# Layer-2 transposes moved from TensorE to DMA, projections moved early, sixth expert ahead of the next scores

## The chip, the core and the metric

The kernel runs on one NeuronCore of a Trainium2 chip. The metric is the device time of one execution in microseconds; the time before is the median of three runs. Engines are called by their short names: PE (TensorE, matmuls and transposes by matmul), DVE (VectorE), ACT (ScalarE), POOL (GpSimd) and SP (SyncE, which here only issues DMAs). Each has its own in-order instruction stream; they meet through semaphores. "Us" are microseconds from the start of the profiled span.

## The reference

A residual network of two layers on x [32 sequences x 64 tokens, 512], with a context of the same shape:

```python
x = x + L0_xattn(layernorm(x), ctx)   # 32 heads of 128, 8 key/value heads, biases
x = x + L0_ffn(layernorm(x))          # relu(x Wup)^2 Wdown + latent experts scaled by top-2 gate; layernorm
x = x + L1_xattn(layernorm(x), ctx)   # rmsnorm inside; 32 heads of 16, 8 key/value heads
x = x + L1_ffn(layernorm(x))
# L1_ffn: logits = x Wg + bg; y_e = relu(x W_e + b_e), e = 0..7; mean of the two experts with the top logits
```

The L1 FFN is computed densely: all 8 experts for every token, then a mask.

## The kernel before

**Numbers.** Each fp32 operand of a matmul is split into two fp16 parts, "hi" (a copy cast to fp16) and "lo" (the remainder); a product is three matmuls (hi hi, hi lo, lo hi), which `group3` issues. So one operand of [128 x 512] takes an ACT copy, a DVE subtraction, and for use as the contracted side eight 128 x 128 transposes (four blocks, two parts).

**Tiles and stages.** The 2048 tokens are 16 tiles of 128 rows (NT = 16), in 4 chunks of 4 tiles (TC = 4). Stages in time: layer-1 attention by head group and chunk (to about 1004 us); layer-1 FFN by chunk (`ffn_chunk(0)` to `ffn_chunk(2)`, then `ffn_last(3)`, in which tiles 0 and 1 of layer-2 attention already run); then `attn_step(n)` for n = 1 to 15, one tile of layer-2 attention each, interleaved with experts of tiles n - 2 and n - 1; last the experts of tile 15. The order of each engine is written out by hand, and the steps below are in that order.

**A layer-2 step on PE** (L1045): experts 6 and 7 of tile n - 2 with `scores(n, 1)` between; `tile_turn` of the normed tile n - 1 (L651 to L661: 8 transposes into a PSUM bank, stored to SBUF by ACT's `tile_store`, L665); `gate(n - 1)`; expert 0; `tile_turn` of the normed tile n + 1; `weigh_v(n, 0)` (probabilities times V, first half); expert 1; `project(n + 1)` (query, key, value); `weigh_v(n, 1)`; expert 2; `turn_o(n)` (attention output turned by PE); expert 3; `output(n)`; expert 4; `scores(n + 1, 0)`; expert 5. Each expert is 12 matmuls of 512 columns into bank 2 or 3 by turns; expert e waits until DVE has evacuated expert e - 2.

**The same step on DVE**: `less_max(n, 0)` (two row maxima L1973, two subtractions L1977), expert 5 of n - 2 (evacuation with bias, L1941), `ffn_lo(n - 1)` (L646: the lo part of the FFN's normed input), expert 6, `row_sums` (L1983), reciprocals, `probs_lo` (L1995), expert 7, `less_max(n, 1)`, `mask_of(n - 1)` (top two of the gate), `row_sums` and `probs_lo` of half 1, expert 0 of n - 1, `out_scale(n, 0)` (L2004), `out_lo` (L2010), reciprocals, expert 1, `norm_stats` of tile n + 2 (L673), `out_scale(n, 1)`, `out_lo`, `q_lo(n + 1)` (L1947), expert 2, `kv_lo(n + 1)` (L1954, L1958, L1963), `norm_apply` (newton from L594, L686) and `tile_lo` (L646) of tile n + 2, expert 3, `add_out(n)` (L2015, residual add and statistics), expert 4, `norm_apply(n)` for the FFN.

**ACT** takes exponentials (L1424) and their fp16 copy (L1430, which waits until the turn of the half before has read the buffer), the relu of each expert with its mask (L1389), `out_hi` (L1443), `project_hi` (L1396 to L1404), `turned_o` (L1448) and the copies of the normed tiles (L651). **POOL** adds experts 1 to 7 into `acc` (L578) and the sum into X (L581).

**SP** already turns queries (two issues, L427), keys (L431) and probabilities (L436) of tiles n >= 2 by DMA: `turn_p(n, 0)`, `store_out(n - 2)`, `turn_p(n, 1)`, `turn_q(n + 1)`, `turn_k(n + 1)`, each behind the semaphores of what it reads and overwrites. `turn_p(n, b)` waits for `probs_lo(n, b)` and for the `weigh_v` before it, since the turned probabilities have one buffer. A turn of probabilities is 16 blocks, one of keys 8.

**The FFN chunk** (L909): 12 jobs of 512 rows, then for each of 4 tiles `ffn_down` and `ffn_fc2`; meanwhile DVE makes the next chunk's normed tiles, and after tiles 0 and 1 PE turns two of them each, through two staging buffers `xs[:, 0]` and `xs[:, 1]`.

Of the kernel before, what the change touches and what calls it, by code (L numbers as in the profile page):

```python
# [22 lines left out]
F16 = mybir.dt.float16  # L23
# [6 lines left out]
P = 128  # L30
# [40 lines left out]
def build(nc, x, ctxT, wB, wX, biasB, bo, gam, bet, lnw, be, bg, w_split, out):  # L71
    with ExitStack() as stack:
# [43 lines left out]
        xs = R4[:, 0:2048].rearrange("p (i s d) -> p i s d", i=2, s=2)  # L116
        XT = R1.rearrange("p (c s k n) -> p c s k n", c=NC, s=2, k=KC)
# [33 lines left out]
        T2 = [parts(R4, 2048, KC, P), parts(R4, 3072, KC, P)]  # L151
        def heads(cols):
            return cols.rearrange("p (h s d) -> p h s d", h=32, s=4)
# [22 lines left out]
        def phalves(cols):  # L176
# [8 lines left out]
                     b_tp=((4, 5), (4, 5)), b_pv=6, b_to=7, b_y=0)  # L185
        TILE1 = REST._replace(qT=qturned(R3[:, 3072:4096].bitcast(F16)), kT=kturned(R3[:, 1024:1536].bitcast(F16)),
# [25 lines left out]
        def home(n):  # L212
            if isinstance(n, int) and n < 2:
                return (TILE0, TILE1)[n]
            return REST
# [4 lines left out]
        const_in, gb_in, out_done = sem("const_in"), sem("gb_in"), sem("out_done")  # L220
# [7 lines left out]
        n_bn, n_mv, n_arg, n_ln, n_r0, n_a, n_a2, n_b, n_r = (sem("n_" + s) for s in "bn mv arg ln r0 a a2 b r".split())  # L228
        n_xn, n_hi, n_lo, n_turned, n_stored = (sem("n_" + s) for s in "xn hi lo turned stored".split())
# [13 lines left out]
        a_q, a_qhi, a_qlo, a_kv, a_kvhi, a_klo, a_kdup = (sem("a_" + s) for s in "q qhi qlo kv kvhi klo kdup".split())  # L243
        q_in, k_in, pr_in = [sem("q_in0"), sem("q_in1")], sem("k_in"), sem("pr_in")
# [11 lines left out]
        wq_in, wkv_in, wo_in, g1_in = sem("wq_in"), sem("wkv_in"), sem("wo_in"), sem("g1_in")  # L256
# [21 lines left out]
        def attn_turn(n):  # L278
            return n * 2 + 31 if not isinstance(n, int) or n > 0 else 28
# [11 lines left out]
        def ffn_turn(n):  # L291
            return n * 2 + 34 if not isinstance(n, int) or n < NT - 1 else 63
# [8 lines left out]
        def _(sp):  # L301
# [66 lines left out]
            sp.dma_start(gamb, gam.broadcast_to([P, D])).then_inc(gb_in, 16)  # L368
            sp.dma_start(betb, bet.broadcast_to([P, D])).then_inc(gb_in, 16)
# [16 lines left out]
            ready(SMALL, 1568, 32, g1w, 0, 32, g1_in)  # L386
# [6 lines left out]
            ready(FC2KV, 1024, 1024, AW, 4096, 1024, wkv_in)  # L393
# [29 lines left out]
            def turn_q(n):  # L423
                sp.wait_ge(a_qlo, n + 1)
                sp.wait_ge(b_s, n * 2)
                for b in range(2):
                    sp.dma_start_transpose(REST.qT[:, b], REST.qs[64 * b:64 * b + 64].rearrange("p h s d -> p (h s d)")).then_inc(q_in[b], 16)  # L427
# [9 lines left out]

            def store_out(n):
# [18 lines left out]
        def _(pool):  # L457
# [112 lines left out]
            g.memset(REST.V[64:P, :, 1, :], 0.0).then_inc(z_ready, 1)  # L570

# [70 lines left out]
        def tile_lo(dve, n, par, src, turned=None):  # L642
# [3 lines left out]
            nc.vector.tensor_tensor(xs[:, par, 1, :], src, xs[:, par, 0, :], ALU.subtract).then_inc(n_lo, 1)  # L646

        def tile_hi(act, n, par, src, turned=None):
            act.wait_ge(n_xn, n + 1)
            w(act, n_turned, n - 1 if turned is None else turned)  # L650
            nc.scalar.activation(xs[:, par, 0, :], src, ACT.Copy).then_inc(n_hi, 1)  # L651
# [52 lines left out]
        def _(pe):  # L704
# [78 lines left out]
            def ffn_job(c, q):  # L783
# [3 lines left out]
                if isinstance(c, int) and c == 0 and kind != UP:  # L787
                    pe.wait_ge(*((fc1_in, 16) if kind == FC1 else (ex_in, 32)))
# [120 lines left out]
            def ffn_chunk(c):  # L909
                n = chunk_first(c)  # L910
                ahead = c == 2
                for q in range(12):
                    ffn_job(c, q)
                    if ahead and q == 6:
                        tile_turn(pe, attn_turn(0), 0, 4, attn_turn(0))
                    if ahead and q == 8:
                        for arrived in (wq_in, wkv_in, wo_in, g1_in):
# [1276 lines left out]
```

## Time and profile before

| | |
|---|---|
| median of 3 runs | 1830.26 us (1821.8 to 1833.26) |
| the profiled execution | 1821.84 us, its span 1820.0 us |
| busy: PE, DVE, ACT, POOL | 1711.9, 1226.9, 758.5, 485.7 us |
| mean granted clock of PE | 0.988 of full |

The span is what the trace covers. A busy PE is not PE at its peak, and idle time of an engine that is not the bound costs nothing; so the views that matter are those that say what each wait waited for. Rows of the timeline overlap a little, since an instruction starts before the last has drained.

### The profile page before, as it was taken

To read this page: it belongs to the slowest core of one execution; us is meant where nothing else is said; L and a number is where in the kernel's file an instruction comes from. 1 tells how busy PE (TensorE), PEld (TensorE's weight loads), DVE (VectorE), ACT (ScalarE), POOL (GpSimd) and SP (SyncE) were. 2 spreads that over 40 slices of the span, in tenths; PEclk is the share of its full clock that TensorE was granted. 3 is DMA by queue.
4 is the path that set the end of the run, shared out by engine and by line. 5 is a ranking of instruction groups with operands and counts; after the bars stand their busy time and mean duration, and the time that the engine had idled before them with its cause. 6 is when DMAs were issued, how large, how long until landed. Compare 5 with 4: busy or idle time off the path is not lost.

```text
span 1820.0 us, 32614 instructions
## 1 busy us (share of the span) xinstructions
PE 1711.9 (94%) x12832; PEld 907.5 (50%) x12832; DVE 1226.9 (67%) x2352; ACT 758.5 (42%) x1335; POOL 485.7 (27%) x370
## 2 busy tenths in 40 slices
PE   5889999999999999999998999998899999999997
PEld 2445555555555555555554444444454444444443
DVE  5776656655665656465657577776878878877863
ACT  5443333333333333333334333343555555545542
POOL 0152650704407025066000000000122322322324
PEclk9899999999999999999999999999999999999999
DMA  6122241412404114035311300002433333333230
GB/s 237 36 59 70 76 145 24 160 27 59 128 13 139 50 45 146 18 93 174 93 37 24 122 1 1 1 1 105 150 71 65 58 65 64 59 65 64 57 66 12
DMA packets 188976, 131.08 MB, mean 72 GB/s; under 512 B 172832, under 2 KB 173088, under 8 KB 180896
## 3 DMA queue, kind: packets, MB, share of 16 engines
q1 hardware_dynamic: 121248, 112.28, 21.4%
q10 hardware_dynamic: 67584, 16.79, 5.3%
q8 instruction: 102, 1.67, 0.4%
q14 instruction: 42, 0.34, 0.1%
HBM read 65.60 MB, written 20.97 MB: 48 GB/s over the span
## 4 chain that ended last, share of the span: by engine, by line
PE 64%; DVE 17%; DMA 7%; ACT 7%; issue 5%; DVEq 0%; ACTq 0%; POOL 0%; SPq 0%; POOLq 0%
PE bank L716 59%; DMA R<-R 7%; PE bank L762 3%; DVE R L1995 2%; DVE smx L1983 2%; ACT R L1430 2%; ACT R L1187 1%; DVE smx L1973 1%; DVE smx L1643 1%; PE bank L658 1%; PE bank L1010 1%; DVE R L1827 1%; ACT R L1338 1%; DVE AW L1645 1%; DVE bank L1977 1%
## 5 line engine op out<-in xcount | busy, mean ns | idle before, releaser
L716 PE MATMUL bank<-R 128*128 128x512 f16 (+1 forms) x7152 | 1298.9, 341 | 22.5 <-DVE R L1590 7.0
L716 PEld LDWEIGHTS bank<-R 128*128 128x128 f16 x7152 | 583.9, 98 | 666.4 <-issue 34.0
L1590 DVE SCALAR_TENSOR_TENSOR R<-bank,biases,R 128x512 f16<-128x512 f32 x288 | 204.7, 746 | 218.7 <-ACT R L1179 176.0
L578 POOL TENSOR_TENSOR R<-R 128x512 f32<-128x512 f32 x112 | 145.3, 1297 | 409.3 <-ACT R L1389 408.0
L1179 ACT ACTIVATE R<-bank,biases 128x512 f16<-128x512 f32 x128 | 87.7, 686 | 255.3 <-PE bank L716 254.5
L469 POOL TENSOR_SCALAR R<-R 128x2048 f32<-128x2048 f32 (+1 forms) x20 | 32.9, 1646 | 416.3 <-PE bank L716 351.5
L1389 ACT ACTIVATE R<-R,msk 128x512 f32<-128x512 f32 x128 | 90.5, 720 | 61.3 <-DVE R L1941 60.7
L716 PE MATMUL bank<-CT,R 128*128 128x512 f16 x384 | 94.2, 398 | 22.9 <-DVE CT L1564 11.5
L1602 DVE SCALAR_TENSOR_TENSOR R<-bank,R 64x512 f16<-64x512 f32 x64 | 44.0, 688 | 98.8 <-ACT R L1187 98.4
L1675 DVE SCALAR_TENSOR_TENSOR X<-bank,X 128x512 f32<-128x512 f32 x128 | 86.8, 683 | 32.2 <-PE bank L716 32.1
L1941 DVE SCALAR_TENSOR_TENSOR R<-bank,R 128x512 f32<-128x512 f32 x128 | 87.0, 680 | 21.4 <-PE bank L716 20.2
L1187 ACT ACTIVATE R<-bank 64x512 f16<-64x512 f32 x128 | 75.7, 591 | 54.0 <-PE bank L716 52.8
L716 PE MATMUL bank<-R,CT 128*128 128x128 f16 x1536 | 91.0, 219 | 0.0
L1214 ACT ACTIVATE AW<-AW 128x512 f32<-128x512 f32 x64 | 40.3, 630 | 120.0 <-DVE AW L1645 120.0
L716 PEld LDWEIGHTS bank<-R,CT 128*128 128x128 f16 x1536 | 88.4, 98 | 0.9
L716 PE MATMUL bank<-AW,R 128*128 128x512 f16 x384 | 88.1, 379 | 0.5 <-ACT R L1448 0.5
L1193 ACT ACTIVATE R<-bank,biases 128x512 f16<-128x512 f32 x128 | 80.8, 685 | 1.1 <-PE bank L762 1.0
L665 ACT ACTIVATE R<-bank 128x1024 f16<-128x1024 f16 x64 | 64.6, 1021 | 39.5 <-PE bank L658 39.5
L483 POOL TENSOR_TENSOR R<-R 128x512 f16<-128x512 f32 x68 | 79.1, 1193 | 1.7
L483 POOL TENSOR_TENSOR AW<-R,AW 128x512 f16<-128x512 f32 x64 | 78.5, 1258 | 1.3
L1219 ACT ACTIVATE AW<-AW 128x512 f16<-128x512 f32 x64 | 40.3, 630 | 82.5 <-DVE AW L1656 82.5
L716 PEld LDWEIGHTS bank<-CT,R 128*128 128x128 f16 x384 | 38.7, 102 | 66.3 <-issue 19.0
(156 smaller groups left out, 1724.3 us busy)
## 6 DMA issues: line engine op xcount, KB each, us to landing
R<-in_wB SPq DMA_DIRECT2D x16, 1024.0 KB, 5.6
R<-in_wX SPq DMA_DIRECT2D x16, 1024.0 KB, 4.8
w_split<-AW SPq DMA_DIRECT2D x16, 1024.0 KB, 4.9
R<-w_split SPq DMA_DIRECT2D x12, 1024.0 KB, 6.9
R<-in_ctxT SPq DMA_DIRECT2D x4, 1024.0 KB, 9.8
X<-in_x SPq DMA_DIRECT2D x4, 1024.0 KB, 13.6
out<-X SPq DMA_DIRECT2D x16, 256.0 KB, 2.0
R<-in_wB SPq DMA_DIRECT2D x7, 512.0 KB, 5.6
```

The source lines that it names most:

```text
L483: last = g.tensor_tensor(lo[:, q], src[:, q], hi[:, q], ALU.subtract)
L578: g.tensor_tensor(acc, acc, tmp[:, e % 2, :], ALU.add).then_inc(e_acc, 1)
L665: nc.scalar.activation(dst, banks16[bank][:, 0:2 * KC * P].rearrange("p (a n) -> p a n", a=2 * KC), ACT.Copy).then_inc(n_stored, 1)
L716: last = pe.matmul(dst, a(sa), b(sb_), start=(k == 0), stop=(k == m - 1))
L762: last = pe.matmul(out_v[:, :, bb, :], V[:, b, p, :], PTb[:, b * 256:(b + 1) * 256], start=(p == 0), stop=(p == 1))
L1179: sc.activation(qT[:, 0, :, j, :], banks[j % 2].rearrange("p (b l) -> p b l", l=64), ACT.Identity, bias=bias_col(g * HG, j)).then_inc(p_hi, 1)
L1187: last = sc.activation(V[64 * half:64 * half + 64, odd:BC:2, 0, :], v[64 * odd:64 * odd + 64], ACT.Copy, scale=UN)
L1193: sc.activation(oT[:, 0, :, jb * P:(jb + 1) * P], banks[6 + jb % 2].rearrange("p (h n) -> p h n", h=HG), ACT.Identity, bias=bias_col(g, 40 ...
L1389: sc.activation(dst, tmp[:, e % 2, :], ACT.Relu, scale=msk[:, 16 + e:17 + e]).then_inc(e_rel, 1)
L1590: v.scalar_tensor_tensor(out=dst, in0=src, scalar=bias, in1=hi, op0=ALU.add, op1=ALU.subtract).then_inc(done, 1)
L1675: v.scalar_tensor_tensor(out=xt, in0=banks[6 + t % 2], scalar=UN2, in1=xt, op0=ALU.mult, op1=ALU.add).then_inc(y_add, 1)
L1941: v.scalar_tensor_tensor(out=tmp[:, e % 2, :], in0=banks[2 + e % 2], scalar=UN, in1=beb[:, e, :], op0=ALU.mult, op1=ALU.add).then_inc(e_bi ...
```

## The change

1. Steady layer-2 steps (n >= 2): the normed tile for the FFN (`turn_ffn`, semaphore `fn_in`) and that for the attention (`turn_attn`, `an_in`) are turned by DMA from SP. The two `tile_turn` of PE and the two `norm_store` of ACT go. Only the attention output is still turned by PE. The turned attention input gets a buffer of its own (TA), the queries a place away from the turned probabilities (LATER, in the first part of the context, which is free by then), V a second buffer for odd tiles.
2. `project(n + 1)` moves ahead of `weigh_v(n, 0)`; `project_hi`, `q_lo` and `kv_lo` move with it. Experts 1 and 2 now lie between the two `weigh_v`, expert 3 behind them, expert 4 behind `turn_o`.
3. On PE, expert 5 of tile n - 1 moves between `output(n)` and `scores(n + 1, 0)`. On DVE and ACT expert 5 of n - 2 moves ahead of `less_max` and of the exponentials. On DVE expert 2 moves ahead of `out_scale(n, 1)`.
4. FFN chunks 0 to 2: the next chunk's four tiles get four staging buffers (`room`) and are turned by four DMAs from SP (`fx_in`); PE's turns and ACT's stores there go.
5. Step 1 becomes `step_one`: PE's turns stay, expert 5 goes ahead of `scores(2, 0)`. Some constant loads share semaphores.

```diff
+        xs_more = R3[:, 3072:4096].bitcast(F16).rearrange("p (i s d) -> p i s d", i=2, s=2)
+        def room(i):
+            return xs[:, i] if i < 2 else xs_more[:, i - 2]
+        TA = parts(R4, 10752, KC, P)
+        V_odd = vhalves(R4[:, 11776:12288])
+        LATER = REST._replace(qs=heads(CT0[:, 0:2048]))
...
 # SP
+            for c in range(NC - 1):
+                sp.wait_ge(u_mm, 12 * (c + 1))
+                for t in range(TC):
+                    sp.wait_ge(n_lo, chunk_first(c) + t + 1)
+                    sp.dma_start_transpose(T1[:, :, :, t * P:(t + 1) * P].rearrange("p s k n -> p (s k) n"),
+                                           room(t).rearrange("p s d -> p (s d)")).then_inc(fx_in[t], 16)
...
+            def turn_norm(n, sem_, par, dst):
+                sp.dma_start_transpose(dst.rearrange("p s k n -> p (s k) n"),
+                                       xs[:, par].rearrange("p s d -> p (s d)")).then_inc(sem_, 16)
+            def turn_ffn(n):
+                sp.wait_ge(n_lo, ffn_stat(n) + 1)
+                if n == 1:
+                    sp.wait_ge(a_kv, 3)
+                else:
+                    sp.wait_ge(e_mm, (n - 1) * NE)
+                turn_norm(n, fn_in, 0, T2[n % 2])
+            def turn_attn(n):
+                sp.wait_ge(n_lo, attn_stat(n) + 1)
+                sp.wait_ge(a_kv, n)
+                sp.wait_ge(b_plo, 4)
+                turn_norm(n, an_in, 1, TA)
...
             turn_k(2)
+            turn_attn(3)
             for n in range(2, NT):
+                turn_ffn(n - 1)
                 turn_p(n, 0)
                 store_out(n - 2)
                 turn_p(n, 1)
                 if n < NT - 1:
                     turn_q(n + 1)
                     turn_k(n + 1)
+                if n < NT - 2:
+                    turn_attn(n + 2)
+            turn_ffn(NT - 1)
...
 # PE, ffn_chunk
-                    if t < 2:
-                        for u in (2 * t, 2 * t + 1):
-                            tile_turn(pe, n + u, u % 2, 4 + u % 2, n + (u - 1))
-                pe.wait_ge(n_stored, n + TC)
+                for landed in fx_in:
+                    pe.wait_ge(landed, (c + 1) * 16)
...
 # PE, steady step (n >= 2), new
+                expert(n - 2, 6, last)
+                scores(n, 1)
+                expert(n - 2, 7, last)
+                gate(n - 1, this)
+                expert(n - 1, 0, this)
+                if more:
+                    project(n + 1, ctx_t, TA)
                 else:
+                    expert(n - 1, 1, this)
+                weigh_v(n, 0)
+                expert(n - 1, 1 if more else 2, this)
                 if more:
+                    expert(n - 1, 2, this)
+                weigh_v(n, 1)
+                expert(n - 1, 3, this)
+                pe.wait_ge(r_lg, n)
+                turn_o(n)
+                expert(n - 1, 4, this)
+                output(n)
+                expert(n - 1, 5, this)
                 if more:
                     scores(n + 1, 0)
...
 # ACT, steady step
+                if two:
+                    expert(n - 2, 5)
                 exponentials(n, 0)
...
+                if two:
+                    if more:
+                        project_hi(n + 1)
                     expert(n - 1, 0)
+                    if not more:
+                        expert(n - 1, 1)
+                    out_hi(n, 0)
+                    if more:
+                        expert(n - 1, 1)
+                        if has(n, -2):
+                            norm_root(act, attn_stat(n + 2), 1)
+                    expert(n - 1, 2)
+                    out_hi(n, 1)
...
 # DVE, steady step
                 if two:
+                    expert(n - 2, 5)
                     less_max(n, 0)
+                    ffn_lo(n - 1)
+                    expert(n - 2, 6)
...
                     expert(n - 1, 0)
+                if two and more:
+                    q_lo(n + 1)
                 out_scale(n, 0)
                 out_lo(n, 0)
                 reciprocals(n, 1)
-                if one:
+                if two and more:
+                    kv_lo(n + 1, not odd)
+                if more:
                     expert(n - 1, 1)
...
                     norm_stats(dve, attn_stat(n + 2), 1, x_tile(n + 2), True)
+                if two:
+                    expert(n - 1, 2)
                 out_scale(n, 1)
                 out_lo(n, 1)
```

## Rows read from the trace of the kernel before

**Rows 1.** Page, busy time; then windows: one layer-2 period, all engines, clock, DMA.
```profile
PE 1711.9 (94%) x12832; PEld 907.5 (50%) x12832; DVE 1226.9 (67%) x2352; ACT 758.5 (42%) x1335; POOL 485.7 (27%) x370
...
core 0: us, PE busy (x) PEld busy (x) DVE busy (x) ACT busy (x) POOL busy (x), PEclk, DMA share, GB/s
...
1519.70:1553.40 33.70, 31.94 (x270) 16.55 (x266) 27.15 (x64) 17.94 (x36) 10.38 (x9) 1.00 0.33 63
```
**Rows 2.** Chain that ended last, 1510 to 1550 us: start us, us, what.
```profile
1512.86 1.30 DVE smx L1973 x2
...
1520.48 4.24 DMA R<-R
1524.81 1.09 ACT R L1430 x2
...
1528.44 4.24 DMA R<-R
1532.72 0.96 PE bank L1010 x32
...
1546.48 1.30 DVE smx L1973 x2
```
**Rows 3.** Timeline of PE: start us, us, instruction, count, idle before and its releaser.
```profile
1499.09 0.96 PE L1010 MATMUL bank<-R 128*128 128x16 f16 x32 [0.51 <-DMA R<-R]
...
1521.10 0.46 PE L716 MATMUL bank<-g1w,R 128*128 128x8 f16 x12 [1.12 <-ACT R L665]
1521.42 2.75 PE L716 MATMUL bank<-R 128*128 128x512 f16 x12
```
**Rows 4.** Timeline of DVE, in two neighbouring periods.
```profile
1503.30 0.28 DVE L1954 TENSOR_TENSOR R<-bank,R 128x128 f16<-128x128 f32 x1
...
1508.93 0.68 DVE L2015 SCALAR_TENSOR_TENSOR X<-bank,X 128x512 f32 x1
1509.77 0.69 DVE L673 BATCH_NORM_STATS2 stat<-X 128x6 f32 x1 [0.15 <-DVE X L2015]
...
1515.99 0.68 DVE L646 TENSOR_TENSOR R<-yn,R 128x512 f16<-128x512 f32 x1
...
1517.74 1.29 DVE L1983 TENSOR_REDUCE smx<-bank 128x8 f32<-128x512 f32 x2 [0.42 <-ACT R L1430]
...
1528.33 0.68 DVE L1941 SCALAR_TENSOR_TENSOR R<-bank,R 128x512 f32<-128x512 f32 x1
```
**Rows 5.** DMA issues: out<-in, queue, kind, count, median us to landing.
```profile
R<-R SPq DMA_TRANSPOSE x70, 4.2
AW<-AW ACTq DMA_TRANSPOSE x64, 3.2
```
**Rows 6.** Timeline around two POOL adds: ACT, POOL and DVE.
```profile
1301.22 1.25 DVE L1963 COPY R<-R 128x384 f16<-128x384 f16 x1
...
1503.42 0.72 ACT L1389 ACTIVATE R<-R,msk 128x512 f32<-128x512 f32 x1 [0.16 <-DVE R L1941]
...
1504.31 1.31 POOL L578 TENSOR_TENSOR R<-R 128x512 f32<-128x512 f32 x1 [4.92 <-ACT R L1389]
1504.41 1.23 DVE L594 TENSOR_TENSOR stat<-stat 128x1 f32<-128x1 f32 x1
```
**Rows 7.** Timeline at the entry (DVE) and at the last tile (DVE, PE).
```profile
1309.63 1.28 DVE L1973 TENSOR_REDUCE smx<-bank 128x8 f32<-128x512 f32 x2
...
1785.11 0.98 DVE L646 TENSOR_TENSOR R<-yn,R 128x512 f16<-128x512 f32 x1 [0.70 <-ACT R L651]
...
1791.96 0.46 PE L716 MATMUL bank<-g1w,R 128*128 128x8 f16 x12 [2.00 <-ACT R L665]
```
**Rows 8.** Timeline of the FFN chunks: DVE at a boundary, PE's transposes at another.
```profile
1071.46 0.69 DVE L1827 TENSOR_TENSOR R<-R 128x512 f32<-128x512 f32 x1 [0.72 <-ACT R L1336]
...
1172.51 1.22 PE L658 MATMUL bank<-ident,R 128*128 128x128 f16 x16 [0.53 <-DVE R L646]
```
**Rows 9.** PE behind its longest layer-2 wait: timeline, then the window after it.
```profile
1601.61 0.96 PE L1010 MATMUL bank<-R 128*128 128x16 f16 x32 [2.13 <-DMA R<-R]
...
1602.40:1606.00 3.60, 3.60 (x16) 1.34 (x14) 1.54 (x3) 2.68 (x9) 0.00 (x0) 0.53 0.00 0
```

More of the change, by code:

```diff
@@ L228, in build @@
         n_bn, n_mv, n_arg, n_ln, n_r0, n_a, n_a2, n_b, n_r = (sem("n_" + s) for s in "bn mv arg ln r0 a a2 b r".split())
+        fx_in = [sem(f"fx_in{t}") for t in range(TC)]
         n_xn, n_hi, n_lo, n_turned, n_stored = (sem("n_" + s) for s in "xn hi lo turned stored".split())
@@ L243, in build @@
         a_q, a_qhi, a_qlo, a_kv, a_kvhi, a_klo, a_kdup = (sem("a_" + s) for s in "q qhi qlo kv kvhi klo kdup".split())
+        fn_in, an_in = sem("fn_in"), sem("an_in")
         q_in, k_in, pr_in = [sem("q_in0"), sem("q_in1")], sem("k_in"), sem("pr_in")
@@ new lines, in step_one @@
+            def step_one(ctx_t):
+                n = 1
+                pe.wait_ge(f_y, NT - 1)
+                tile_turn(pe, ffn_stat(0), 0, 7, ffn_turn(0))
+                turn_p(n, 0)
+                gate(0, T2[0])
+                expert(0, 0, T2[0])
+                pe.wait_ge(r_lg, n)
+                tile_turn(pe, attn_stat(2), 1, 7, attn_turn(2))
+                weigh_v(n, 0)
+                expert(0, 1, T2[0])
+                turn_p(n, 1)
+                project(2, ctx_t, T2[1])
+                weigh_v(n, 1)
+                expert(0, 2, T2[0])
+                turn_o(n)
+                expert(0, 3, T2[0])
+                output(n)
+                expert(0, 4, T2[0])
+                expert(0, 5, T2[0])
+                scores(2, 0)
@@ new lines, in attn_step @@
+            def attn_step(n, ctx_t):
+                more = n < NT - 1
+                last, this = T2[n % 2], T2[1 - n % 2]
+                expert(n - 2, 6, last)
[5 more added lines that the diff above has]
+                    project(n + 1, ctx_t, TA)
+                else:
+                    expert(n - 1, 1, this)
+                weigh_v(n, 0)
+                expert(n - 1, 1 if more else 2, this)
+                if more:
+                    expert(n - 1, 2, this)
+                weigh_v(n, 1)
+                expert(n - 1, 3, this)
+                pe.wait_ge(r_lg, n)
+                turn_o(n)
+                expert(n - 1, 4, this)
+                output(n)
+                expert(n - 1, 5, this)
+                if more:
@@ L1085, in attn_step @@
                     scores(n + 1, 0)
-                expert(n - 1, 5, T2[1 - buf])
             def ctx_tile(n):
@@ L1458, in attn_step @@
                 if two:
-                    expert(n - 2, 5)
                     expert(n - 2, 6)
-                if one:
-                    norm_store(ffn_turn(n - 1), 1 - buf)
+                if not two:
+                    norm_store(ffn_turn(0), 0)
                 if two:
@@ L1494, in attn_step @@
                     expert(n - 1, 4)
-                tile_hi(act, ffn_stat(n), 0, yn, ffn_turn(n - 1) + 1 if one else 33)
+                if two:
+                    act.wait_ge(fn_in, (n - 1) * 16)
+                tile_hi(act, ffn_stat(n), 0, yn, ffn_turn(0) + 1)
             def ffn_last(c):
@@ L2049, in attn_step @@
                     expert(n - 1, 0)
+                if two and more:
+                    q_lo(n + 1)
+                if two and not more:
+                    expert(n - 1, 1)
                 out_scale(n, 0)
@@ L2059, in attn_step @@
                     norm_stats(dve, attn_stat(n + 2), 1, x_tile(n + 2), True)
+                if two:
+                    expert(n - 1, 2)
                 out_scale(n, 1)
                 out_lo(n, 1)
-                if more:
+                if not two:
                     q_lo(n + 1)
-                if one:
                     expert(n - 1, 2)
-                if more:
                     kv_lo(n + 1)
@@ L2136, in _ @@
             ffn_last(NC - 1)
-            attn_step(1)
-            with dve.Fori(2, NT - 2) as n:
-                attn_step(n)
-            attn_step(NT - 2)
-            attn_step(NT - 1)
+            attn_step(1, True)
+            with dve.Fori(0, NT // 2 - 2) as i:
+                for k in range(2):
+                    attn_step(i * 2 + (2 + k), k == 1)
+            attn_step(NT - 2, False)
+            attn_step(NT - 1, True)
             ffn_lo(NT - 1)
```

190 lines of the change are left out of this document (79 added, 111 removed).

## The prediction

> **What bounds the kernel now.** I began with the page's shares. TensorE (PE) is busy for 94% of the span, and its granted clock is nearly full [rows 1], which invites the reading "PE is the bound, so every transpose taken off it is time won". The change acts in three stages, so I looked at each: the FFN chunks of layer 1 (about 1004 to 1215 us), the attention steps of layer 2 (n = 2 to 14, from 1309.6 us on) and the last tile.
>
> In layer 2 the work repeats. The row maxima of tile n's first half (`less_max(n, 0)`, L1973) begin at 1512.86 and, a step later, at 1546.48 [rows 2]: a period of 33.63 us. The shares give PE 31.94 us in such a period [rows 1]. The chain of waits [rows 2] is the view that decides. It doesn't run along PE. From L1973 it goes through DVE and ACT to a DMA transpose of 4.24 us (the first half's probabilities, turned from 1520.48), ACT's L1430, which may overwrite the buffer only then, DVE again, a second DMA transpose (from 1528.44), then PE's `weigh_v(n, 1)` and what follows it (an expert, `turn_o`, expert, output, expert), then DVE and L1973 of the next tile. This is a closed loop: each link waits for the one before. I call the start of L1973 L, and the start of `weigh_v(n, 1)` V. [rows 2] give V = L + 1532.72 - 1512.86 = L + 19.86.
>
> **The steady step, what PE no longer does.** Both PE transposes (L658, 8 blocks each) and the store behind them leave: 2 x 8 x 0.056 = 0.9 us of issue, the 1.12 us for which the gate waits on ACT's L665 [rows 3], and some gaps. What is left on PE, start to start: ten groups of twelve 512-wide matmuls at 2.59 (25.9; the 2.75 of a row less 0.16 that overlaps the next), the key/value projection at half that width 1.31, gate 0.31, `weigh_v` 2 x 0.82, `turn_o` 0.44, scores 2 x 0.44 [rows 3]: 30.5 us. If PE were the bound, a step would fall by 3.1.
>
> **The same step, walked along the loop.** From L to the second transpose nothing leaves the loop. `expert(n-2, 5)` used to be evacuated inside it, but there DVE waited for ACT anyway (0.42 us in front of L1983 [rows 4]); with it gone DVE waits 1.1. So V stays L + 19.86.
> From V on PE used to run expert, `turn_o`, expert, output, expert. Now it is `weigh_v` 0.82, expert 3 2.59, `turn_o` 0.44, expert 4 2.59, output 2.59 and 0.16 for the last to drain [rows 3]: output is there at V + 9.2. DVE then needs 3.93 from its residual add (L2015 at 1508.93) to the next L1973 [rows 4]. Before, it came to that add at V + 9.84 (1499.09 to 1508.93 [rows 3, 4]), held up by the query and key/value remainders; these move ahead of V, which wins 0.6. But expert 5 now stands in front of `less_max`: its evacuation, 0.60 (L1941's 0.68 less the overlap with what follows [rows 4]), is now on the loop, which costs 0.6. Sum: 19.86 + 9.23 + 3.93 + 0.60 = 33.62, against 33.63. **The loop takes back all that PE gives.** PE will instead wait in front of the gate: `ffn_lo` ends at L + 3.2 (less_max 2.53, then L646 0.68 [rows 4]), and the DMA transpose that replaces PE's comes behind it. Its price isn't shown for this form. It is 8 blocks; ACT's transposes of 8 blocks land in 3.2 us and SP's of 16 in 4.2 [rows 5]. I take 3.3 and keep 4.2 as the upper end. The gate starts at L + 6.55. Then gate, expert 0 and the projections, 6.8, `weigh_v(n, 0)` 0.82 and two experts 5.18: `weigh_v(n, 1)` could start at L + 19.35, 0.5 before V. The gate's stall thus stays hidden.
>
> **A new collision.** Between the second transpose and V the new DVE order is, from L + 15.47: expert 0 0.6, `q_lo` 0.6, `out_scale` 0.4, ACT's copy 0.5, `out_lo` and reciprocals 0.5, `kv_lo` 1.11 (L1954 to L594), expert 1 0.6, `norm_stats` 1.25 (L673 to L1941), expert 2 0.6, `out_scale(n, 1)` [rows 4]. Expert 2 is delivered at L + 21.7. ACT's relu of it starts at a = L + 21.75, and GpSimd's add (L578) at a + 0.88 (1503.42 to 1504.31 [rows 6]). ACT's copy of the attention output follows the relu at a + 0.62, `out_lo` (L2010) at a + 1.07. L2010 reads two tiles in SBUF, and so does L594: that one starts 0.1 us behind an L578 and takes 1.23 instead of 0.15, ending 0.02 behind it; a copy (L1963) that falls behind an L578 takes 1.25 instead of 0.26 [rows 6]. In each case the work proper began 0.13 to 0.14 before the end of GpSimd's instruction. So `out_lo` will end at a + 0.88 + 1.27 - 0.14 + 0.43 = a + 2.44 = L + 24.2, where PE wants to start `turn_o` at V + 3.41 = L + 23.27. That is 0.97 later on the loop, in the 12 steps n = 2 to 13 that norm a tile n + 2 (step 14 has no `norm_stats`, so `out_lo` meets expert 1's add and is through at L + 22.4, before PE asks). The period becomes 34.6. The meeting has a margin of only 0.19 us (1.07 - 0.88).
> The Trainium skill (SBUF — State Buffer, section "SBUF: two separate sides") states the rule more strictly: whichever of the two engines starts first holds the shared ports for the whole instruction. By that `out_lo` would start at GpSimd's end, 0.14 later, 1.7 us more over 12 steps; the rows above show it starting earlier, so the sum goes by them.
>
> **Where steps begin and end.** Entry: in step 1 the scores of tile 2 now follow expert 5. Expert 5 would start at about 1307.4 and be there at 1310.15, so L of tile 2 comes at 1310.75 instead of 1309.63 [rows 7]: +1.1. Tail: the last tile's gate waits 2.00 us for turn and store and starts at 1791.96, 2.6 after expert 7 has freed PE (0.6 of it the transpose); `ffn_lo` ended at 1786.09, so a turn of 3.3 lands at 1789.4 [rows 7]: -2.4 or so.
>
> **The FFN chunks.** At each of three boundaries four tiles were turned by PE while it ran at full load: 2 groups x 16 transposes x 0.056 = 1.8 us (a row of 16 has 1.22 with its drain [rows 8]). DVE's y loop follows closely: the next chunk's first job came to DVE at 1071.46, 0.72 behind the last y [rows 8], so PE's gain passes only as far as DVE is earlier too. DVE loses its wait for ACT's fourth copy (I estimate 0.9, from DVE's 0.7 and ACT's 0.6 an instruction) and the 0.72, and then stands at the job at 1069.8: 1.7 earlier. The turns by DMA (four, about 1.9 of issue and 3.3 to land each) are issued from 1052 and down by 1062, before PE needs them at 1066. Third boundary: 0.53 of wait in front of the turn as well [rows 8], 2.3. Together -5.5; if DVE holds PE at each, -3.
>
> **Sum.** 12 x 0.97 = +11.6; +1.1; -2.4; -5.5: +4.8 on the profiled execution's 1821.84 (its span is 1820.0): 1826.6. The median of the runs is 1830.26, 8.4 above the profiled one, and the same sum on it gives **1835 us**, 0.3% more. SP now issues seven transposes a step, at most 1.9 each: 13 us of 34, and none in front of a probability turn: the FFN's is issued at L + 3.25, the next at L + 7.6. ACT's new waits (`an_in`, `fn_in`) ask for turns that landed 10 us and more before.
>
> **Rivals.**
> *No meeting.* If L2010 gets in ahead of L578, or expert 2 is delivered 0.2 us otherwise, the period stays 33.6: 1830.3 + 1.1 - 2.4 - 5.5 = 1823.5. For it: the margin of 0.19. Against it: both starts hang on the same delivery.
> *The FFN turn becomes the loop* (slower). It decides once the gate comes later than L + 7.1 (without the meeting; L + 8.0 with it). If the turn takes 4.24, the gate starts at L + 7.5. PE has by then idled some 2.6 to 3 us. With 1.6 for that, V = L + 7.5 + 6.8 + 1.6 + 6.0 = L + 21.9, `turn_o` at L + 25.3, and the next L 10.35 later (0.44 + 5.18 + 0.20 + 3.93 + 0.60): 35.65. 13 x 2.0 = +26.3, net +19.5: 1850. The slow clock alone only brings `turn_o` to where the meeting has it: 34.8. Against it: transposes of the same size land in 3.2.
> *PE is the bound after all* (faster): 13 steps of 30.5, -41 - 5.5 - 2.4: 1781. For it only the 94%; against it the chain, in which every link has its semaphore.
>
> **How the numbers follow.** Forecast with the meeting 0.45; no meeting 0.22; the FFN turn on the loop 0.22; PE as the bound 0.07; something unlisted 0.04. The likeliest gives 1835. The range goes from 1815 (no meeting, and 8 us of the spread that the runs before show, 1821.8 to 1833.3) to 1856 (the FFN turn on the loop and 6 us), and leaves PE's case and a late tail outside. A measurement of this kernel can tell about 1% (18 us) from no change. Faster by over 1%: PE's case and a little of the second, 0.11. Slower by over 1%: most of the third (1848.6 is its edge) and a tail of the first, 0.25. Within 1%: 0.64.
>
> **What would show it.** In the changed profile: starts of L1973's first half 34.6 apart; PE waiting 2.5 us or more in front of the gate, on a DMA; the second `weigh_v` still waiting on its DMA; `out_lo`'s row at about 1.4 us instead of 0.43 beside an L578, with `turn_o` waiting on it by 0.9; no wait at the chunk boundaries. I am wrong in the walk if the period is under 33.4, in the meeting if it is 33.6, and in the turn's price if the gate starts later than L + 7.1 and the second `weigh_v` follows PE, not its DMA.

## The result, and the profile after

The changed kernel takes 1833.3 us (median of 20 runs, 1828.97 to 1838.58) beside 1825.91 for the kernel before in the same comparison (20 runs, 1819.66 to 1833.26): a ratio of 1.004, 95% interval 1.0028 to 1.0053. The forecast was 1835 and "within 1%"; both came out. Of the 7.4 us by which it is slower, the sum had 4.8. The profiled execution took 1831.48, its span is 1829.7; before it was 1821.84 and 1820.0, so the pair of profiles to be explained differs by 9.7.

The page of the changed kernel (busy time, share of the span, instructions), and its first DMA queue:

```profile
PE 1705.9 (93%) x12512; PEld 891.6 (49%) x12512; DVE 1226.7 (67%) x2352; ACT 720.6 (39%) x1295; POOL 484.6 (26%) x371
...
q1 hardware_dynamic: 163488, 122.77, 24.3%
```

PE lost its transposes in the second layer and at the chunk boundaries, and yet it is busy for only 93% of a longer span. The engine that was relieved waits more. The same window view as in [rows 1], over one period of the changed kernel, from one start of the first half's maxima (now L2043) to the next:

```profile
1481.41:1516.41 35.00, 31.16 (x251) 15.50 (x249) 26.87 (x64) 16.04 (x35) 10.42 (x9) 1.00 0.40 76
```

The period is 35.00 us (33.70 in the window of [rows 1]) and PE is idle for 3.84 of it (1.76 before). The starts of L2043, first half, are 1306.77, 1341.64, 1376.66, 1411.54, 1446.55, 1481.41, 1516.41, 1551.30, 1586.29, 1621.16, 1656.17, 1691.03, 1725.87 and 1763.02: twelve steps of 34.84 to 35.02 (mean 34.93), and 37.15 for tile 14.

Where PE waits in that stretch, by its timeline (start, duration, what, count, idle time before and its releaser); this answers to [rows 3]:

```profile
1501.49 0.96 PE L1055 MATMUL bank<-R 128*128 128x16 f16 x32 [0.61 <-DMA R<-R]
...
1505.83 0.61 PE L1065 MATMUL bank<-ident,R 128*128 128x128 f16 x8 [0.77 <-DVE R L2080]
...
1522.72 0.46 PE L763 MATMUL bank<-g1w,R 128*128 128x8 f16 x12 [2.32 <-DMA R<-R]
1523.03 4.44 PE L763 MATMUL bank<-R 128*128 128x512 f16 x12
...
1537.19 0.95 PE L1055 MATMUL bank<-R 128*128 128x16 f16 x32
...
1540.85 0.61 PE L1065 MATMUL bank<-ident,R 128*128 128x128 f16 x8
```

The first two are the second `weigh_v` (V, at L + 20.08) and `turn_o` (L + 24.42) of the step that begins at 1481.41. The loop's DMA transposes end last at V, and `turn_o` waits for `out_lo` (L2080). The other four belong to the next step, L = 1516.41: the gate waits 2.32 us for the FFN norm's turn, expert 0 behind it takes 4.44 us instead of 2.75, and V (L + 20.78) and `turn_o` (L + 24.44) come without any wait. There are steps of both kinds: of the twelve gates between 1347 and 1733 all wait for that DMA, 2.19 to 2.41 us, and six are followed by a slow expert. `turn_o` comes at the same time in both. Behind a slow expert PE would have been ready for it 3.40 us behind V, at 1540.59, as it is in the steps of `e2_late` below; `out_lo` ended at 1540.70, so it is `out_lo` that holds `turn_o` there as well, by a quarter of a microsecond instead of 0.77:

```profile
1539.33 1.37 DVE L2080 TENSOR_TENSOR R<-R 128x256 f16<-128x256 f32 x1 [0.73 <-ACT R L1498]
```

The meeting, then, is there in both kinds of step. ACT's copy, POOL's add and DVE's `out_lo`, which answer to [rows 6]:

```profile
1503.88 0.40 ACT L1498 ACTIVATE R<-R 128x256 f16<-128x256 f32 x1
...
1504.14 1.26 POOL L625 TENSOR_TENSOR R<-R 128x512 f32<-128x512 f32 x1 [0.65 <-ACT R L1442]
...
1504.31 1.37 DVE L2080 TENSOR_TENSOR R<-R 128x256 f16<-128x256 f32 x1 [0.76 <-ACT R L1498]
```

The subtraction took 1.37 us; the one of the first half, with no add beside it, took 0.43 (at 1499.01). It ended at 1505.68, 0.28 behind the add's end at 1505.40. The chain of waits, from one L to the next, answers to [rows 2] (start, duration, what):

```profile
1481.49 1.21 DVE smx L2043 x2
...
1489.02 4.30 DMA R<-R
1493.40 1.09 ACT R L1485 x2
...
1495.72 1.28 DVE R L2065 x2
1497.00 0.60 DVE R L2009
...
1502.52 0.70 DVE R L2009
1503.25 0.72 ACT R L1442
1503.97 0.31 ACT R L1498
1504.31 1.38 DVE R L2080
1505.69 0.14 issue
1505.83 0.61 PE bank L1065 x8
1506.43 5.19 PE bank L763 x24
1511.76 0.70 DVE X L2085
```

The loop is there, through the first probability turn. The second turn, which was in the chain of before, has dropped out: between 1495.72 and `out_lo` DVE's own order, expert 2's relu and the meeting are what ends last.

The difference of the profiles by stage:

| stage | before | after | difference |
|---|---|---|---|
| up to the first FFN job of layer 1 (code not touched) | 1004.06 | 1006.38 | +2.3 |
| from there to the scores of tile 1 | 269.24 | 263.17 | -6.1 |
| step 1 (to L of tile 2) | 36.33 | 37.22 | +0.9 |
| steps 2 to 13 | 408.32 | 419.10 | +10.8 |
| step 14 | 33.50 | 37.15 | +3.65 |
| the last tile | 68.55 | 66.68 | -1.9 |

In steps 2 to 13 the kernel before had lost 4.7 us to two late steps (35.04 and 36.95 instead of 33.63), so the steady steps cost 15.5 (12 times 1.29 to 1.30), and 10.8 is what this pair of profiles shows.

### The profile page after: what moved, and what is told of

It reads as the page before. It is cut to its first block, busy times and chain, and to the rows that moved or that the text cites. A ratio compares the mean times of both kernels' runs of the same rounds, so it can differ in the third digit from the quotient of the medians.

```text
span 1829.7 us, 31948 instructions
## 1 busy us (share of the span) xinstructions
PE 1705.9 (93%) x12512; PEld 891.6 (49%) x12512; DVE 1226.7 (67%) x2352; ACT 720.6 (39%) x1295; POOL 484.6 (26%) x371
## 4 chain that ended last, share of the span: by engine, by line
PE 65%; DVE 19%; ACT 5%; issue 5%; DMA 4%; ACTq 1%; DVEq 0%; POOL 0%; SPq 0%; POOLq 0%
PE bank L763 61%; DMA R<-R 3%; PE bank L809 3%; DVE smx L2043 1%; ACT R L1242 1%; DVE R L2009 1%; DVE stat L720 1%; DVE R L693 1%; DVE R L2065 1%; DVE smx L2053 1%; PE bank L1055 1%; DVE R L1895 1%; DVE smx L1711 1%; ACT R L1485 1%; ACTq L1280 1%
## 5 line engine op out<-in xcount | busy, mean ns | idle before, releaser
L763 PE MATMUL bank<-CT,R 128*128 128x512 f16 x384 | 94.0, 397 | 22.9 <-DVE CT L1632 11.6
L809 PE MATMUL bank<-AW,R 128*128 128x256 f16 x512 | 67.4, 275 | 4.2 <-DMA AW<-AW 2.6
```

The source lines that it names most:

```text
L763: last = pe.matmul(dst, a(sa), b(sb_), start=(k == 0), stop=(k == m - 1))
L809: last = pe.matmul(out_v[:, :, bb, :], V[:, b, p, :], PTb[:, b * 256:(b + 1) * 256], start=(p == 0), stop=(p == 1))
```

## The experiments

Seven kernels ran, six edits and the kernel before once more. Each states its edit on the changed kernel, if nothing else is said. `expert(n, e)` on DVE evacuates the bank in which PE left expert e and adds the bias; on ACT it is the relu with the gate's weight.

**Is it the meeting?** (`e2_late`) The sixth experts stay where they are; only expert 2's evacuation goes behind `out_lo`, on DVE and on ACT:

```diff
-                if two:
-                    expert(n - 1, 2)
                 out_scale(n, 1)
                 out_lo(n, 1)
+                if two:
+                    expert(n - 1, 2)
```

> The changed kernel with one thing moved: on DVE and ACT expert 2 is handled behind out_lo(n, 1) instead of ahead of out_scale(n, 1). Theory (loop with the meeting): out_lo no longer falls behind GpSimd's add of expert 2, its row goes back from 1.37 to 0.43 us, turn_o no longer waits (0.77), and the period falls from 34.9 to about 33.9, that is by 1.0 in 12 steps: 12 us less than the changed kernel, ratio to the kernel before about 0.998. Rival (the 2.3 us stall in front of the gate and the slow clock behind it set the period): neither changes, the period stays 34.8 to 34.9, ratio 1.004. Rival (PE's own work sets the period): no change either.

1823.51 us (12 runs), ratio 0.9994 (0.9981 to 1.0007): level with the kernel before, and 0.5% under the changed one. The direction is as expected; the size is 8 to 9 us where 12 were expected. The mean period is 34.10: ten steps of 33.94 to 34.15, and 34.32 and 34.47 in the two steps in which expert 0 ran at the lower clock. The timeline of this kernel, in the step that begins at 1507.54:

```profile
1527.64 0.96 PE L1055 MATMUL bank<-R 128*128 128x16 f16 x32 [0.85 <-DMA R<-R]
...
1529.55 0.43 DVE L2080 TENSOR_TENSOR R<-R 128x256 f16<-128x256 f32 x1 [0.48 <-ACT R L1498]
```

`out_lo` is back at 0.43 us, PE's wait for it is gone from the timeline, and the wait in front of V is now PE's last on the loop. So the meeting costs about 0.83 a step (34.93 to 34.10). The edit also takes expert 2's evacuation, 0.6 us of DVE, from in front of `out_lo`; but that is not what the changed kernel lacked: there `out_lo` started at 1504.31, and with 0.43 us it would have ended at 1504.74, before PE is ready for `turn_o` at V + 3.40 = 1504.89. Without the meeting the loop stands at 34.10, not at the 33.6 of the rival "no meeting": 0.5 of the walk was missing (below).

**Is it expert 5 in front of the maxima?** (`e2e5_late`) On top of the last kernel, expert 5's evacuation goes behind `less_max(n, 0)` and `ffn_lo`, and on ACT behind the exponentials:

```diff
-                    expert(n - 2, 5)
                     less_max(n, 0)
                     ffn_lo(n - 1)
+                    expert(n - 2, 5)
                     expert(n - 2, 6)
```

> As e2_late, and on DVE and ACT expert 5 of n - 2 is handled behind less_max(n, 0) and ffn_lo, where DVE waits 1.1 us for ACT anyway; PE is as in the changed kernel. Theory (loop): the 0.6 us of expert 5 leaves the loop as well, period 33.3, some 7 us less than e2_late and 19 less than the changed kernel: ratio to before about 0.994. Rival (stall in front of the gate): expert 5 off the loop brings the gate's transpose 0.6 earlier, so that one gives 0.6 too, but then from 34.9 to 34.3: ratio 1.000.

1820.16 us (12 runs), ratio 0.9973 (0.9958 to 0.9989). Faster than the last kernel by 3.4 us where 7 were expected, and the period is 34.2 in ten steps and 33.4 to 33.5 in two. The expectation, 33.3, missed, and by the number alone the rival (34.3) did better; but the gate no longer waits in this kernel, so the rival's reason isn't there either. The link was cut, and the time came back elsewhere. Its timeline, L at 1513.31:

```profile
1516.44 1.28 DVE L2008 SCALAR_TENSOR_TENSOR R<-bank,R 128x512 f32<-128x512 f32 x2
...
1517.18 4.45 PE L763 MATMUL bank<-R 128*128 128x512 f16 x12 [1.88 <-DVE R L2008]
...
1521.76 0.69 DVE L2008 SCALAR_TENSOR_TENSOR R<-bank,R 128x512 f32<-128x512 f32 x1 [0.85 <-PE bank L763]
...
1522.37 1.28 DVE L2042 TENSOR_REDUCE smx<-bank 128x8 f32<-128x512 f32 x2
```

Expert 5 and expert 7 share a bank. PE stood for 1.88 us until expert 5 had left it, ran expert 7 in 4.45 us instead of 2.75, and DVE, which evacuates expert 7 before the second half's maxima, waited 0.85 for it. The second half's maxima start at L + 9.06 instead of L + 8.09 (1481.41 to 1489.50 in the changed kernel). What expert 5 gave at one end of the loop, expert 7 took in its middle. What took it is the lower clock: in the step that begins at 1615.90 expert 7 waits almost as long, runs at the full clock, the second half's maxima start at L + 8.09 again, and the period is 33.47, near the loop's 33.3:

```profile
1619.76 2.76 PE L763 MATMUL bank<-R 128*128 128x512 f16 x12 [1.84 <-DVE R L2008]
```

**Is it the gate's wait and the clock behind it?** (`ffn_first`) The gate waits longest, so the tempting mend is to send the FFN norm's remainder first:

```diff
                     expert(n - 2, 5)
-                    less_max(n, 0)
                     ffn_lo(n - 1)
+                    less_max(n, 0)
                     expert(n - 2, 6)
```

> The changed kernel with ffn_lo(n - 1) ahead of less_max(n, 0) on DVE, so that the FFN turn is issued 2.5 us earlier in the step. Theory (loop): the wait in front of the gate (2.32) goes, the granted clock stays full in the step, and it is still no faster: ffn_lo's 0.6 to 0.8 us now stand in front of less_max on the loop, period 35.5, ratio to before about 1.008. Rival (the stall in front of the gate with the slow clock behind it sets the period): 2.3 to 4 us less per step, period 31 to 33, ratio 0.975 to 0.99.

1847.83 us (4 runs), ratio 1.0124 (1.0106 to 1.0141), period 35.95 (1522.94 to 1558.89): the loop theory's direction, and worse than its 35.5 and 1.008. Two of PE's waits in that kernel, the gate's and the longest:

```profile
1526.13 0.45 PE L763 MATMUL bank<-g1w,R 128*128 128x8 f16 x12 [0.16 <-DMA R<-R]
...
1530.67 2.75 PE L763 MATMUL bank<-AW,R 128*128 128x512 f16 x12 [1.48 <-DVE R L2065]
```

The gate's wait is gone (0.16), the matmuls behind it run at the full clock, the profile's mean clock rose from 0.981 to 0.988, and the kernel is 0.8% slower than the changed one. `ffn_lo` took 0.94 instead of 0.68 in its new place, all of it in front of the maxima, and the period grew by 1.02. `turn_o` starts at 1547.35, that is L + 24.41, where the changed kernel has L + 24.42. So PE's largest wait and its slow clock stood beside the loop: taking them away won nothing, and PE waits elsewhere instead, 1.48 us in front of the projections for `probs_lo`.

**Has the gate's wait room to grow?** (`ffn_twice`) The FFN norm's turn is done twice, one behind the other, with the same values, and who waits for it waits for the second:

```diff
                 turn_norm(n, fn_in, 0, T2[n % 2])
+                sp.wait_ge(fn_in, n * 32 - 16)
+                turn_norm(n, fn_in, 0, T2[n % 2])
```

> The kernel after, with the FFN norm's turn done twice, one behind the other (the second overwrites the first with the same values), so that it lands 3.3 us plus an issue later, about 3.5 to 4.5 us. Theory 1 (the loop with the meeting sets 34.94; the gate's wait of 2.32 us lies beside it, and TensorE has 0.61 us left ahead of weigh_v(n,1)): the gate waits 6 to 7 us, the spare 0.6 is used up, and the period rises by the rest, 2.9 to 3.9 us, to 38 to 39; the run takes 1870 to 1885 us. Theory 2 (the gate's wait has room to grow, since the experts' work ahead of weigh_v can be caught up): period 35 to 36, the run 1835 to 1848 us.

1887.61 us (one run; 1870 to 1885 were expected), mean period 38.4 over eleven steps (1352.02 to 1774.41), within the 38 to 39 expected. PE in the step that begins at 1505.58:

```profile
1515.23 0.48 PE L765 MATMUL bank<-g1w,R 128*128 128x8 f16 x12 [5.54 <-DMA R<-R]
1515.57 4.25 PE L765 MATMUL bank<-R 128*128 128x512 f16 x12
...
1529.54 0.95 PE L1057 MATMUL bank<-R 128*128 128x16 f16 x32
```

The gate comes at L + 9.65 instead of L + 6.31, 3.34 later, and V at L + 23.96, without any wait in front of it. From the gate on PE sets the pace: 20.78 (V of the changed kernel's steps with a slow expert) + 3.34 - 0.19 (4.25 instead of 4.44 for expert 0) = 23.93. The step grew by 3.5. There is the rival "the FFN turn becomes the loop", made by hand, and the gate's wait has hardly any room: 0.8 us up to V where PE keeps its full clock (0.6 of it in the row above), none where it doesn't. It was hidden in the changed kernel because the meeting held `turn_o` a quarter of a microsecond longer than the slow clock did; without the meeting it shows, in the two longer steps of `e2_late`.

**What are the chunks worth alone?** (`chunks_only`) The FFN chunks turned by DMA, the second layer as before.

```diff
-                        for u in (2 * t, 2 * t + 1):
-                            tile_turn(pe, n + u, u % 2, 4 + u % 2, n + (u - 1))
-                pe.wait_ge(n_stored, n + TC)
+                for landed in fx_in:
+                    pe.wait_ge(landed, (c + 1) * 16)
```

> The kernel before with part 4 of the change alone: the FFN chunks' tiles turned by DMA. Theory: -6 us as between the two traces' chunk stages (boundaries 1.8, 1.6, 2.6), steady period 33.63 as before, ratio 0.9967. Rival (the two traces differ there by chance, DVE holds the chunks): 0 to -3 us, ratio 0.9985 or more.

1824.56 us (12 runs), ratio 0.9997 (0.9982 to 1.0012). Expected was 0.9967, a gain of 6 us, and the interval leaves room for 3.3 at most. In its profile the boundaries are as short as in the changed kernel: the same jobs stand 57.14 us apart across the first of them (1045.17 to 1102.31) and 37.60 across the second (to 1139.91), where before has 58.97 and 39.21 (1040.30, 1099.27, 1138.48), and the stage from the first FFN job to the scores of tile 1 is 4.6 us shorter than before. But its first FFN job starts at 1008.93 where the profile of before has 1004.06, and its last stage took 71.8 us against 68.55, both in code that it doesn't change. So the saving is seen in the stage and isn't seen in the medians. The last stage can be accounted for: its first probability turn took 5.9 us instead of 4.2 and PE waited 2.13 us for it (0.47 in before), which is 1.7, and the run of 96 matmuls behind the last gate took 22.57 instead of 20.88, again 1.7. Steps 2 to 13 took 409.6 us (408.3 in before), with four late turns. None of that is code that the edit changes, and the next run shows what such late turns have in common. Whether they eat the saving in every run, I can't say from one profile. The first layer varies by itself: the first FFN job started anywhere from 1002.35 to 1010.21 in the nine profiles.

**The kernel before once more** (`before2`), for its late steps.

> The kernel before once more, for its profile. Theory 1 (a step is late where an instruction fetch of 16 KB on one DMA engine falls into the transfer of turn_p(n,1); where it falls depends on the phase of the code, so it is about the same in each run): period 33.63 with two or three steps of 35 to 37 us, in steps that need not be those of the first profile; each late step has its landing at 5 us or more instead of 4.24, and a fetch of queue 8 within that transfer; the steps on time have their fetch before or behind it. Theory 2 (late steps come from something else): late steps without a fetch inside the transfer. The first FFN job of the second layer starts anywhere from 1002 to 1009, since the first layer's code is the same in all kernels and varied by that much.

1824.43 us. Its period is 33.63 again, with two late steps again: 34.93 (from 1446.84) and 35.28 (from 1582.65). I looked at the DMA traffic around each step's two probability turns in both profiles of before. The DMA view shows busy tenths and GB/s in 40 slices, and the instruction fetches as queue 8. First the late turn of step 1477.82 in the first profile (window 1485 to 1492), then the turn in the same place one step on (1519 to 1526), which was on time:

```profile
DMA  0000000005999999999999400000069899991000
GB/s 0 0 0 0 0 0 0 0 0 111 230 219 217 202 199 218 217 211 200 293 208 41 1 0 3 7 9 10 9 140 297 178 222 351 386 374 35 0 0 0
...
q8 instruction: 1, 0.02, 0.8%
...
R<-R SPq DMA_TRANSPOSE x1, 5.6
```

```profile
DMA  0000000000000005999999999999940000000599
GB/s 0 0 0 0 0 0 0 0 0 0 0 0 0 0 0 123 225 217 218 209 208 218 212 215 219 222 217 183 218 93 0 0 0 0 0 0 0 222 374 398
...
R<-R SPq DMA_TRANSPOSE x1, 4.2
```

In the late one the flow breaks off early, and a trickle of 3 to 10 GB/s follows for about 1 us before the turn counts as landed, after 5.6 us instead of 4.2. A fetch of 0.02 MB falls into exactly that stretch. I counted packets and fetches by half microseconds for both turns of the 13 steps in both profiles of before: of 52 turns, four landed late (5.6, 5.9, 5.6 and 5.9 us), and each of the four has a fetch in the last microsecond of its transfer; none of the other 48 has one inside its transfer. `chunks_only` has five late turns from step 2 to the last tile: three of 5.5 to 5.9 us with such a fetch, and two of 4.9 us with a fetch of 0.01 MB (queue 14) near the end of the transfer. That bears out Theory 1 as a coincidence without exception. No run moved a fetch on purpose, so the cause stays inferred.

**A loop that is opened.** (`scores_early`) The last kernel follows from the chain. In `e2_late` the scores are done at 1505.7 and the maxima start at 1507.54, because add, statistics, expert 4, norm and expert 5 stand in front of them on DVE; and the scores stand behind `output` on PE, because both use bank 0. The projections now come early, so nothing else keeps the scores there. Edits on `e2_late`: the output goes to bank 4, PE issues `scores(n+1, 0)` before `output(n)`, DVE takes the maxima before the add, ACT the exponentials before the norm's root. Expert 6 of n - 2 also moves on DVE, behind `probs_lo(n, 0)`. The parts were not tried one by one.

```diff
-b_to=7, b_y=0)
+b_to=7, b_y=4)
...
                 expert(n - 1, 4, this)
+                if more:
+                    scores(n + 1, 0)
                 output(n)
                 expert(n - 1, 5, this)
-                if more:
-                    scores(n + 1, 0)
...
+                if two and more:
+                    less_max(n + 1, 0)
                 add_out(n)
```

> The kernel e2_late, and beyond it: the output of tile n goes to bank 4 instead of bank 0, so that scores(n+1,0) no longer waits for add_out(n); PE issues scores(n+1,0) before output(n), and VectorE and ScalarE take less_max(n+1,0) and its exponentials ahead of add_out(n) and the FFN norm. In e2_late scores(n,0) are done at 1505.7 and the maximum starts only at 1507.54, since 4.65 us of VectorE work (add_out, statistics, expert 4, norm, expert 5) stand ahead of it, and scores(n,0) themselves stand behind output(n), which waits for turn_o. Theory 1 (the period is the loop from the maximum over V, out_lo, turn_o and output back to the maximum, and TensorE has 2.3 + 0.8 us of idle time in it): with the maximum out of that loop the period falls from 34.10 to what TensorE needs, 30.5, plus a fetch wait of up to 1, so 31 to 32; 13 steps give -27 to -40 us on e2_late, ratio to before 0.977 to 0.985. Theory 2 (TensorE itself is the bound, and its waits only shift): period 34, ratio 0.999. Theory 3 (the transposing DMAs queue up, since the FFN's turn and the weights' turn now come together): period 33 to 35, with waits for DMA of over 3 us ahead of weigh_v.

1783.79 us (4 runs, 1779.33 to 1790.57) against 1824.44, ratio 0.9783 (0.9749 to 0.9816): faster than both kernels, by about 40 and 50 us, though the interval leaves open whether the gain on the kernel before reaches 2%. PE's waits over one period by its timeline, then the window view of that period:

```profile
1529.70 2.76 PE L763 MATMUL bank<-R 128*128 128x512 f16 x12 [0.40 <-DVE R L2015]
...
1535.66 0.46 PE L763 MATMUL bank<-g1w,R 128*128 128x8 f16 x12 [0.17 <-DMA R<-R]
```

```profile
1523.61:1554.97 31.36, 30.80 (x249) 15.43 (x248) 26.71 (x63) 16.24 (x34) 10.49 (x8) 1.00 0.46 85
```

The period is 31.36 here (31.36 to 31.81 in the steps from 1335.64 on, mean 31.46), PE works through 30.80 of it at the full clock, and its remaining waits are 0.40 and 0.17. The prediction had PE's own work at 30.5 a step. The time that the change takes off PE was real; it was locked up behind the loop. Whether the kernel before could be opened in the same way wasn't tried: there the projections come later, and PE's 31.94 of work in a period of 33.70 leaves at most 1.76 a step.

## Why the prediction was right, and where it was off

**Which bound.** "The loop takes back all that PE gives": confirmed. Moving DVE's order moved the period (34.93, 34.10, 35.95), relieving PE's gate did not help, and once the loop was opened the period fell to PE's 30.80 plus 0.56.

**The meeting.** Predicted: expert 2 delivered at L + 21.7, POOL's add 0.88 behind ACT's relu, `out_lo` ending at L + 24.2, `turn_o` waiting 0.9 to 0.97. Measured: 1502.52 + 0.60 is L + 21.71; 0.89; L + 24.27; 0.77; and 0.83 a step when it is taken away. The Trainium skill (SBUF — State Buffer, section "SBUF: two separate sides") has the one engine lock the other out for its whole instruction. Here L2080 ended 0.28 behind the add, and its uncontended row is 0.43, so it did not wait for the add's end: the trace disagrees by about 0.15 us, as the rows of before did, as far as GpSimd's spans, which the profile gives only roughly, can show it.

**The period, 34.93 instead of 34.6.** The terms that were too small are handovers. `turn_o` was put at L + 24.24 (23.27 + 0.97) and came at L + 24.42: ACT's relu started 0.13 behind expert 2's delivery, where I took 0.05, and PE started 0.15 behind `out_lo`'s end, where I took 0.05 (+0.18 together). From `turn_o` to the next L it is 10.58 (1505.83 to 1516.41) where I had 10.35: output is there 5.93 behind `turn_o` instead of 5.82, and DVE needs 4.65 from add to maxima, not 4.53 (+0.23). 34.59 + 0.41 = 35.00, that step's period. V itself came 0.22 late (from the second turn's issue to V it is 4.46 us, where before has 4.28), which matters only without the meeting: 20.10 + 3.41 + 10.58 = 34.09, and `e2_late` measured a mean of 34.10. So "no meeting" would have been 34.1 and not 33.6.

**Step 14.** The sum gave it nothing, and it cost 3.65. This is the step of the argument that missed something. `turn_p(14, 1)` was issued at 1741.49, and V came at 1747.69, L + 21.82. PE's timeline and the DMA view of the changed kernel, 1744 to 1748:

```profile
1747.69 0.96 PE L1055 MATMUL bank<-R 128*128 128x16 f16 x32 [2.55 <-DMA R<-R]
...
1748.50 4.44 PE L763 MATMUL bank<-R 128*128 128x512 f16 x12
```

```profile
GB/s 220 207 220 228 202 228 220 182 159 202 192 208 182 182 184 164 307 154 108 82 59 23 8 0 0 0 10 8 8 10 10 8 10 56 287 287 289 289 262 289
...
q8 instruction: 1, 0.02, 1.5%
```

The same trickle, with the fetch in it; the turn landed after 6.2 us. It is no chance of one profile: in `e2_late`, `e2e5_late`, `ffn_first` and `ffn_twice` the same turn of step 14 took 6.0 to 6.2 us too, each time with a fetch 2.0 us before V (in `e2_late` V at L + 21.79, the step 37.12), and in `scores_early`, where the fetch falls 4.6 us before V, PE didn't wait. So V came 1.7 late; expert 3 behind the long wait ran at the lower clock, and V to the next L took 15.33 where `e2_late`'s steady steps have 14.0, 1.3 more; the missing 0.5 of the walk makes up the rest (33.50 + 0.5 + 1.7 + 1.3 = 37.0). Why the fetch of step 14 falls there in five kernels, no run shows. The prediction had seen the late landings of before ([rows 9] has one) and took them for something that both kernels share and that drops out of the difference.

**The FFN turn.** Predicted: 3.3 to land, gate at L + 6.55, at least 2.5 of idle. Measured: gate at L + 6.31, idle 2.32. So the turn is, if anything, cheaper than taken. The step that failed is "the gate's stall thus stays hidden": with the lower clock behind it V comes at L + 20.78, 0.7 later than where its DMA lands, and PE is ready for `turn_o` only 0.26 before the meeting lets it go. The sentence in the rival, "The slow clock alone only brings `turn_o` to where the meeting has it", is nearly what happened in half of the steps. The Trainium skill (TensorE: Matmul & The Clock Gate, "HAM oscillation") warns of waits for DMA in a loop that bring the lower clock back each time round; here it came back in six of twelve.

**Ends and chunks.** Entry +0.9 (predicted +1.1); tail -1.9 (-2.4), with the last gate starting right behind expert 7 and no wait; chunks 1.8, 1.6 and 2.7 at the three boundaries (1.7, 1.7, 2.3). PE now runs through the first boundary without a break, 180 matmuls in a row; its wait for DVE ahead of it is the same 0.91 as before (there at 1040.30):

```profile
1042.62 39.18 PE L763 MATMUL bank<-R 128*128 128x512 f16 x180 [0.91 <-DVE R L1897]
```

**The total.** The change was mis-sized by 2.6 (+4.8 against +7.4), and the base of 1830.26, a median of three, was 4.35 above the one of twenty. The two errors have opposite signs; that is why 1835 lies within 2 us of 1833.3. The 2.6 is itself small by luck. By the rows the steady steps cost 15.5 where the sum had 11.6, and step 14 3.65 where it had nothing; with entry, tail and chunks that is 15.5 + 3.65 + 0.9 - 1.9 - 6.1 = 12.1. Against it stand the late steps of the kernel before, 4.7 us in one profile and 3.0 in the other, of which the changed kernel has none in steps 2 to 13: about 8 is left, near the 7.4 of the medians. So the late landings did nearly drop out, but only because step 14 of the one kernel costs about what two late steps of the other do. The direction and the class follow from the working, the last 2 us don't.

## What to carry to other kernels

Close the loop before counting an engine's work: start at one instruction, follow the chain of waits to the same instruction of the next tile, and ask of each edit whether it is on that path. Taking work off an engine at 94% bought nothing, and mending its largest wait made it worse, while a kernel that moves one half of the scores past an output they did not depend on was 2.2% faster (1.8 to 2.5). If a bank or a place in an order closes the loop rather than a value that is needed, that is what to change first.

## What the runs showed of the hardware

**An instruction fetch can go with a late transpose.** Where a fetch of 0.02 MB falls into the end of a 16-block DMA transpose, a trickle of 3 to 10 GB/s follows and the landing is 1.4 to 1.7 us later in before, 1.6 to 1.8 in step 14 of five changed kernels. At the beginning of the transfer (step 1656.17 of the changed kernel) a trickle followed as well, of 9 to 19 GB/s for some 0.6 us, but the flow then came back at 280 to 297 GB/s, together with the next turn's, and the transfer landed after 4.5 us, against 4.4 without it.

**The length of a wait does not tell the clock behind it.** In the changed kernel, the step at 1481.41 has 2.41 us of idle time in front of the gate and the next one 2.32. Windows behind the two:

```profile
1488.20:1491.00 2.80, 2.80 (x21) 1.32 (x18) 2.77 (x6) 0.72 (x1) 0.57 (x2) 1.00 0.30 60
```

```profile
1523.00:1527.50 4.50, 4.50 (x20) 1.72 (x18) 4.31 (x9) 1.07 (x2) 2.07 (x3) 0.62 0.57 107
```

Behind the longer wait the granted clock was 1.00, behind the shorter 0.62, that is the lower level (1.2 GHz) for most of the stretch. In `e2e5_late` an idle time of 1.88 was followed by the lower clock, and one of 1.84 in the same place was not. What decides stays open; what it costs is about 1.7 us each time (4.44 against 2.75 for twelve matmuls).
